# Second attention's scores: two heads at a time, the low key parts against the high query parts alone

## The chip, the cores and the metric

The kernel runs on one core of one Trainium2 chip. The metric is the device time of one execution in microseconds (us), as the median of several runs. The core has a matrix engine (PE, with its weight loads listed apart as PEld), a vector engine (DVE), a scalar engine (ACT), a pool engine (POOL) and a DMA queue issued by SP. Every engine takes its own instructions in program order; semaphores order them against each other.

## The reference

One layer on x of 16 sequences x 512 tokens x 256 channels, all in f32: `x = x + attention1(layernorm(x))`, then `x = x + block2(layernorm(x))`. Block 2 starts with the attention that the change touches:

```
q = (x @ Wq).reshape(b, t, H, D)                 # 16 heads of 64
q = concat(q_nope, rope(q_rope))                 # 32 + 32
k = concat(kv, rope(k_rope))                     # folded here: one key of 64, shared by all heads
att = softmax(causal(q . k / sqrt(64)))          # 512 x 512 scores for each head
y = (att @ v) @ Wo
x = x + y; then 8 experts (2 chosen) and one shared
```

## The kernel before

One pass of the loop handles one sequence (`sequence(b, last)` on each engine), 16 in all. The first attention, the projections, the second attention (`attend(b, 1, last)`) and the experts follow each other. The kernel is written engine by engine; the order on each engine is the order of the code, and `Signal` objects are semaphores with a count per sequence.

The second attention goes by units. A unit `u` is one group `g` of four heads and one tile `j` of 128 query tokens (`j` = 0, 1, 2, 3), so there are 4 x 4 = 16 units in a sequence. In turn PE makes the scores of unit u+1 (`score`), transposes the softmax numerators of unit u (`transpose_prob`, L670, 128x128 f32) and weighs the values of unit u-1 (`weigh_values`, L681, whose four heads stand in four 32-column tiles of the array). The scores of head `q` go to PSUM bank `q`. DVE takes the row maximum of each head (L1192), ACT the exponentials (L953), and PE's next scores into bank `q` wait for that head's exponentials (`prob_ready`).

Precision is kept by splitting. A query of 64 numbers is split in a high part (ACT, the copy into `stq` that signals `qh_ready`) and the low rest (DVE, L1324), stacked as 128 rows (high, low) by a transpose into `qt`. The high key part stands twice in `khh` (rows 0 to 63 and 64 to 127), the low key part twice in `kll`. `score` with `a == 1` issues three matmuls for a head: `qt` x `khh` (L657), `qt` x `kll` (L658), both with all 128 rows and m columns of keys, m = max(128(j+1), 256), and then the causal mask as a bf16 matmul of 128 columns (`ident16` x `mask16`, L659), whose end raises `s_psum`. Every matmul of the program has a weight load of its own.

Of the kernel before, what the change touches and what calls it, by code (L numbers as in the profile page):

```python
# [23 lines left out]
F32 = mybir.dt.float32  # L24
F32R = mybir.dt.float32r
BF16 = mybir.dt.bfloat16
ALU = mybir.AluOpType
# [3 lines left out]
P = 128  # L31
NB, L, C = 16, 512, 256
NT = L // P
KC = C // P
H = 16
D = C // H
HP = 32
G = 4
NG = H // G
M = 1  # L40
NM = G // M
# [4 lines left out]
DK = 2 * R  # L46
# [3 lines left out]
UNITS = NG * NT  # L50
# [23 lines left out]
def tile_of(u):  # L74
    return ORDER[u % NT]
# [24 lines left out]
def _build(nc, ctx, dram):  # L100
# [4 lines left out]
    def at(name, shape, dt, offset):  # L105
        return nc.alloc_sbuf_tensor_at(name, shape, dt, offset=offset)
# [23 lines left out]
    ident16 = new("ident16", [P, P], BF16)  # L130
    mask16 = new("mask16", [P, P], BF16)
# [53 lines left out]
    qkt = new("qkt", [SD, 2 * H, L], BF16)  # L185
    qt = at("qt", [P, H, L], F32R, region_q)
# [15 lines left out]
    qf = at("qf", [P, 2, 8, DK], F32, o + 8192)  # L202
    ta = at("ta", [P, 2, 8, R], F32, o + 12288)
    tb = at("tb", [P, 2, 8, R], F32, o + 14336)
    stq = at("stq", [P, 2, 8, 2, DK], F32R, o + 16384)

    va = new("va", [P, NT, H, HP], F32)
    xn0 = at("xn0", [P, NT, C], F32, place[0])
    sg = at("sg", [P, 2, L], F32, place[0])
    khh = new("khh", [P, L], F32R)  # L210
    kll = new("kll", [P, L], F32R)
# [27 lines left out]
    bank = [scores[:, i] for i in range(4)]  # L239
# [57 lines left out]
    qh_ready = Signal(sem("qh_ready"), 2 * NT)  # L297
    ql_ready = Signal(sem("ql_ready"), 2 * NT)
# [4 lines left out]
    s_psum = Signal(sem("s_psum"), 2 * NM * UNITS)  # L303
    negmax_ready = Signal(sem("negmax_ready"), 2 * NM * UNITS)
    prob_ready = Signal(sem("prob_ready"), 2 * G * UNITS)
# [255 lines left out]
    def _(pe):  # L561
        mm = nc.tensor.matmul
# [67 lines left out]
        def transpose_quad(b, n):  # L630
# [11 lines left out]
                                          stk[:, t % 2, quad * 8 + i].rearrange("p s d -> p (s d)"), ident16[:, :])  # L642
            ins.then_inc(stackt_psum.sem, 1)

        def score(b, a, u, part):
            g, j = u // NT, tile_of(u)
            n = (j + 1) * P
            for q in range(M * part, M * part + M):
                h = g * G + q
                if u > 0:  # L650
                    pe.wait_ge(prob_ready.sem, prob_ready.at(b, (a * UNITS + u - 1) * G + q + 1))
                if a == 0:
                    mm(bank[q][:, 0:n], qkt[:, h, j * P:(j + 1) * P], qkt[:, H + h, 0:n], start=True, stop=False)  # L653
                else:
                    m = max(n, 2 * P)
                    tok = qt[:, h, j * P:(j + 1) * P]
                    mm(bank[q][:, 0:m], tok, khh[:, 0:m], start=True, stop=False)  # L657
                    mm(bank[q][:, 0:m], tok, kll[:, 0:m], start=False, stop=False)  # L658
                ins = mm(bank[q][:, n - P:n], ident16[:, :], mask16[:, :], start=False, stop=True)  # L659
            ins.then_inc(s_psum.sem, 1)  # L660

# [31 lines left out]
        def attend(b, a, last):  # L693
            if a == 0 and b == 0:
                for part in range(NM):
                    score(b, a, 0, part)
            for u in range(UNITS):
                if u + 1 < UNITS:
                    for part in range(NM):
                        score(b, a, u + 1, part)  # L700
                if u == 0:
                    if a == 0:
                        pe.wait_ge(down_added.sem, down_added.at(b, 0))
                        pe.wait_ge(stackt_act.sem, stackt_act.at(b, 4 * NT))
                    else:
                        pe.wait_ge(qt_act.sem, qt_act.at(b, 2 * NT))
                        pe.wait_ge(qt_dve.sem, qt_dve.at(b, 2 * NT))
                        pe.wait_ge(vb_ready.sem, vb_ready.at(b, 1))
                early = EARLY[tile_of(u)]
                transpose_prob(b, a, u, range(early))  # L710
                if u > 0:
                    weigh_values(b, a, u - 1)
                    if u % NT == 0:
                        transpose_sums(b, a, u // NT - 1)
                transpose_prob(b, a, u, range(early, tile_of(u) + 1))
            transpose_sums(b, a, NG - 1)
            weigh_values(b, a, UNITS - 1)

            project_out(b, a, range(NG - 2))
            if a == 1 and not last:  # L720
                transpose_first(b + 1)
            project_out(b, a, range(NG - 2, NG))
# [87 lines left out]
        def sequence(b, last):  # L810
            if b == 0:
                pe.wait_ge(stackt_act.sem, stackt_act.at(b, 4 * NT))
            attend(b, 0, last)

            keep_busy(8, 6)
            transpose_tokens(b, 1, (0, 1))
            keep_busy(2, 6)
            hi_split(b, 1, 1)
            for n in range(2 * NT):
                project_q(b, n)  # L820
                if n == 0:
                    transpose_tokens(b, 1, (2, 3))
                if n == KV_STEP:
                    project_kv(b)
                if n > 1:
                    transpose_q(b, n - 2)
                if n == KV_STEP + 3:
                    pe.wait_ge(kv_copied.sem, kv_copied.at(b, 1))
                    settle(pe, pe_passed)
                    for t in range(NT):  # L830
                        ins = nc.tensor.transpose(bank[6][:, t * R:(t + 1) * R], kf[0:R, t * P:(t + 1) * P], ident[0:R, 0:R])
                    ins.then_inc(vb_psum.sem, 1)
            pe.wait_ge(kll_ready.sem, kll_ready.at(b, 1))
            pe.wait_ge(nope_ready.sem, nope_ready.at(b, 2 * NT))
            pe.wait_ge(rot_ready.sem, rot_ready.at(b, 2 * NT))
            for part in range(NM):
                score(b, 1, 0, part)
            transpose_q(b, 2 * NT - 2)
            transpose_q(b, 2 * NT - 1)
            attend(b, 1, last)  # L840

            if not last:
                for t in range(2):
                    project_qk(b + 1, t)
                    project_v(b + 1, t)
            transpose_tokens(b, 2)
            hi_split(b, 2)

            for m, (x_, w_) in enumerate(TERMS):
                if m == 2:  # L850
                    lo_split(b, 2)
                for k in range(KC):
                    ins = mm(bank[3][0:E, :], wgate[:, w_, k], XT[x_][:, k], start=m == 0 and k == 0, stop=m == 2 and k == KC - 1)
            ins.then_inc(gatet_psum.sem, 1)
            gate_up(b, 0, (0,))
            pe.wait_ge(gatet_copied.sem, gatet_copied.at(b, 1))
            settle(pe, pe_passed)
            for t in range(NT):
                ins = nc.tensor.transpose(bank[2][:, t * E:(t + 1) * E], lgt[0:E, t * P:(t + 1) * P], ident[0:E, 0:E])
            ins.then_inc(gate_psum.sem, 1)  # L860
            gate_up(b, 0, (1,))
            for e in range(NE + 1):
                if not last:
                    if e in PROJECT_AT:
                        project_qk(b + 1, PROJECT_AT[e])
                        project_v(b + 1, PROJECT_AT[e])
                    for n in QUADS_AT.get(e, ()):
                        transpose_quad(b + 1, n)
                if 1 <= e < NE:
                    spread_comb(b, e)  # L870
                if e + 1 < NE:
                    gate_up(b, e + 1)
                if e == NE and not last:
                    pe.wait_ge(hid_ready.sem, hid_ready.at(b, NE))
                    for part in range(NM):
                        score(b + 1, 0, 0, part)
                if e == 0:
                    transpose_comb(b)
                else:
                    down(b, e - 1)  # L880
# [14 lines left out]
    def _(act):  # L895

        def copy(out, in_, **k):
            return nc.scalar.activation(out, in_, ACT.Copy, **k)  # L898
# [95 lines left out]
        def sequence(b, last):  # L994
# [3 lines left out]
            for n in range(2 * NT + 3):  # L998
# [11 lines left out]
                if 1 <= n <= 2 * NT:  # L1010
                    act.wait_ge(rope_ready.sem, rope_ready.at(b, n))
                    act.wait_ge(nope_ready.sem, nope_ready.at(b, n))
                    if n >= 3:
                        act.wait_ge(qt_psum.sem, qt_psum.at(b, 2 * (n - 2)))
                    copy(stq[:, (n - 1) % 2, :, 0], qf[:, (n - 1) % 2]).then_inc(qh_ready.sem, 1)
                if n == 2 * NT:
                    for part in range(NM):
                        exps(b, 1, 0, part)
# [70 lines left out]
    def _(dve):  # L1089
# [194 lines left out]
        def sequence(b, last):  # L1284
# [24 lines left out]
            for n in range(2 * NT + 3):  # L1309
# [11 lines left out]
                if 1 <= n <= 2 * NT:  # L1321
                    dve.wait_ge(qh_ready.sem, qh_ready.at(b, n))
                    s = (n - 1) % 2
                    tt(stq[:, s, :, 1], qf[:, s], stq[:, s, :, 0].bitcast(F32), ALU.subtract).then_inc(ql_ready.sem, 1)  # L1324
                if 3 <= n < 3 + NT and not last:
                    ins = first_stats(b + 1, n - 3)
                if n == 3 + NT and not last:
# [148 lines left out]
```

## Time and profile before

| | |
|---|---|
| median of 3 runs | 3697.05 us (3696.23 to 3699.96) |
| the profiled execution's own time | 3699.16 us |
| its span, from first to last instruction | 3697.5 us |
| PE busy (matmul) | 3354.6 us, 91% of the span |
| PEld busy (weight load) | 2632.8 us, 71% |
| DVE, ACT, POOL busy | 75%, 65%, 29% |
| mean granted TensorE clock | 0.993 |
| matmuls L657, L658, and masks L659 (of both attentions) | 1024, 1024, 2048 |

A matmul's busy time includes the time until its result has left the array, and matmuls overlap. So what a matmul costs the stream is not its duration, but the distance from its start to that of the next one, called its turn below. Weight loads run beside the matmul ahead of them where they can.

### The profile page before, as it was taken

How to read it: one execution, taken by the hardware profiler on the slowest of the kernel's cores; microseconds unless marked ns; L12 is line 12 of the kernel's file. 1: busy time of each engine (PE TensorE's matmuls, PEld its weight loads, DVE VectorE, ACT ScalarE, POOL GpSimd, SP SyncE). 2: the span in 40 equal slices, each digit the busy share in tenths (PEclk: the TensorE clock that was granted, in tenths of full speed). 3: DMA queues.
4: the chain of work that ended last, by engine and by line, in shares of the span. 5: the costliest groups of instructions: out<-in, count | busy, mean ns of one | idle time of the engine just before them, and what ended most of it. 6: DMA issues, size and time to landing. Idle time of an engine off the chain costs nothing.

```text
span 3697.5 us, 82731 instructions
## 1 busy us (share of the span) xinstructions
PE 3354.6 (91%) x31744; PEld 2632.8 (71%) x31744; DVE 2763.8 (75%) x5950; ACT 2406.8 (65%) x6426; POOL 1085.9 (29%) x778
## 2 busy tenths in 40 slices
PE   2599999999999999999999999999999999999998
PEld 2477677776767777677776767777677776767776
DVE  3676877878777776877778777777877778777775
ACT  1666667666676766667666676766667666676764
POOL 0424222242412424222242412424222242412420
PEclk9799999999999999999999999999999999999999
DMA  3000000000000000000000000000000000000000
GB/s 80 1 7 1 13 2 7 7 7 7 1 13 2 7 7 1 13 1 7 7 7 7 1 13 2 7 7 1 13 2 7 7 7 7 2 13 2 7 2 7
DMA packets 33766, 28.95 MB, mean 8 GB/s; under 512 B 8864, under 2 KB 33312, under 8 KB 33376
## 3 DMA queue, kind: packets, MB, share of 16 engines
q1 hardware_dynamic: 33376, 23.68, 2.2%
q8 instruction: 253, 4.15, 0.5%
q14 instruction: 137, 1.12, 0.1%
HBM read 15.28 MB, written 8.39 MB: 6 GB/s over the span
## 4 chain that ended last, share of the span: by engine, by line
PE 71%; ACT 14%; DVE 10%; issue 3%; POOL 1%; SPq 1%; DMA 0%; ACTq 0%; POOLq 0%; DVEq 0%
PE bank L670 14%; PE scores L782 11%; PE bank L681 8%; ACT prob L953 6%; PE scores L657 5%; PE bank L806 5%; PE scores L733 4%; PE scores L658 4%; PE scores L756 3%; PE bank L617 3%; PE bank L641 3%; PE scores L659 3%; DVE negmax L1192 2%; ACT qkt L898 2%; PE scores L653 1%
## 5 line engine op out<-in xcount | busy, mean ns | idle before, releaser
L953 ACT ACTIVATE prob<-scores,negmax 128x128 f32<-128x128 f32 (+3 forms) x2048 | 1057.8, 535 | 186.3 <-DVE negmax L1192 180.6
L1192 DVE TENSOR_REDUCE negmax<-scores 128x1 f32<-128x128 f32 (+3 forms) x2048 | 872.6, 481 | 56.9 <-PE scores L659 42.4
L670 PE MATMUL bank<-ident,prob 128*128 128x128 f32 x5120 | 725.6, 279 | 50.6 <-DVE probt L1200 43.6
L1200 DVE COPY probt<-bank 128x512 f32<-128x512 f32 x896 | 596.1, 683 | 171.0 <-PE bank L670 165.3
L670 PEld LDWEIGHTS bank<-ident,prob 128*128 128x128 f32 x5120 | 544.1, 141 | 163.6 <-issue 66.6
L659 PE MATMUL scores<-mask,ident 128*128 128x128 bf16 x2048 | 438.1, 225 | 0.0
L953 ACT ACTIVATION_READ_ACCUMULATOR prob<-scores,negmax 128x1 f32 x2048 | 436.1, 213 | 0.0
L657 PE MATMUL scores<-khh,qt 128*128 128x256 f32 (+2 forms) x1024 | 416.3, 407 | 13.3 <-POOL kll L545 13.3
L486 POOL TENSOR_TENSOR otl<-onm,oth 128x512 fp32r<-128x512 f32 x96 | 122.6, 1277 | 888.8 <-ACT oth L898 888.8
L497 POOL TENSOR_TENSOR rq<-ssq,expo 128x32 f32<-128x32 f32 x64 | 359.9, 5632 | 39.6 <-DVE ssq L1163 39.6
L481 POOL COPY rexp<-rsum 128x512 f32<-128x512 f32 x128 | 78.0, 610 | 981.8 <-DVE rsum L1204 981.8
L898 ACT ACTIVATE probt<-bank 128x512 f32<-128x512 f32 x384 | 232.8, 606 | 198.8 <-PE bank L670 198.8
L782 PE MATMUL scores<-xth,wgu 128*128 128x512 f32 x1152 | 335.9, 413 | 0.0
L658 PE MATMUL scores<-kll,qt 128*128 128x256 f32 (+2 forms) x1024 | 331.4, 324 | 0.0
L659 PEld LDWEIGHTS scores<-mask,ident 128*128 128x128 bf16 x2048 | 199.5, 97 | 135.8 <-issue 110.5
L653 PE MATMUL scores<-qkt 96*128 96x128 bf16 (+3 forms) x1024 | 261.1, 304 | 29.3 <-ACT prob L953 6.6
L898 ACT ACTIVATE qkt<-bank 96x1024 bf16<-96x1024 bf16 x256 | 243.7, 1015 | 66.5 <-PE bank L641 66.5
L782 PEld LDWEIGHTS scores<-xth,wgu 128*128 128x128 f32 x1152 | 215.6, 189 | 41.8 <-issue 0.3
L641 PE MATMUL bank<-ident,stk 128*128 128x128 bf16 x2048 | 146.8, 224 | 87.1 <-ACT qkt L898 59.2
L657 PEld LDWEIGHTS scores<-khh,qt 128*128 128x128 f32 x1024 | 203.1, 198 | 18.8 <-POOL kll L545 17.1
L806 PE MATMUL bank<-wd,hidh 128*128 128x256 f32 x1152 | 211.5, 283 | 1.8 <-DVE hidl L1378 1.8
L1373 DVE TENSOR_TENSOR sg<-scores,sg 128x512 f32<-128x512 f32 x144 | 99.1, 688 | 134.0 <-ACT sg L1049 134.0
(187 smaller groups left out, 6654.6 us busy)
## 6 DMA issues: line engine op xcount, KB each, us to landing
x_in<-in_x_rows SPq DMA_DIRECT2D x16, 512.0 KB, 3.8
out_rows<-x SPq DMA_DIRECT2D x16, 512.0 KB, 2.9
r_gu<-in_wg SPq DMA_DIRECT2D x2, 512.0 KB, 5.0
r_gu<-in_wu SPq DMA_DIRECT2D x2, 512.0 KB, 5.7
r_d<-in_wd SPq DMA_DIRECT2D x1, 1024.0 KB, 7.1
r_wqt<-in_wq_nope_t SPq DMA_DIRECT2D x1, 512.0 KB, 6.7
r_wqr<-in_wq SPq DMA_DIRECT2D x2, 256.0 KB, 8.3
r_wob<-in_wo SPq DMA_DIRECT2D x1, 512.0 KB, 5.3
```

What stands on the lines that cost most here:

```text
L497: nc.gpsimd.tensor_tensor(rq[:, s], ssq[:, s], expo[:, 0:1].to_broadcast([P, 2 * H]), ALU.pow).then_inc(rq_ready.sem, 1)
L653: mm(bank[q][:, 0:n], qkt[:, h, j * P:(j + 1) * P], qkt[:, H + h, 0:n], start=True, stop=False)
L657: mm(bank[q][:, 0:m], tok, khh[:, 0:m], start=True, stop=False)
L658: mm(bank[q][:, 0:m], tok, kll[:, 0:m], start=False, stop=False)
L659: ins = mm(bank[q][:, n - P:n], ident16[:, :], mask16[:, :], start=False, stop=True)
L670: ins = nc.tensor.transpose(bank[4 + n % 2][:, q * P:(q + 1) * P], prob[:, u % 2, q, i * P:(i + 1) * P], ident[:, :])
L782: ins = mm(bank[2 * s + w][:, :], wgu[:, w_, e, k, w * I:(w + 1) * I], XT[x_][:, k], start=m == 0 and k == 0, stop=m == 2 and k == KC - 1)
L806: ins = mm(bank[4 + t // 2][:, (t % 2) * C:(t % 2 + 1) * C], (hidh, hidl)[x_][:, s, t * P:(t + 1) * P], wd[:, w_, e], start=e == 0 and m = ...
L898: return nc.scalar.activation(out, in_, ACT.Copy, **k)
L953: nc.scalar.activation(prob[:, u % 2, q, 0:n], bank[q][:, 0:n], ACT.Exp, bias=negmax[:, a, u, q:q + 1], accum_out=sums[:, a, u, q:q + 1]). ...
L1192: nc.vector.tensor_reduce(negmax[:, a, u, M * part:M * part + M], scores[:, M * part:M * part + M, 0:n], axis=AX.X, op=ALU.max, negate=Tru ...
L1200: nc.vector.tensor_copy(probt[:, u % 2, i], bank[4 + n % 2][:, :]).then_inc(probt_dve.sem, 1)
```

## The change

Three things change for the second attention. (1) In `stq`, odd heads are stacked (low, high) instead of (high, low): `high_low(s)` gives the views, and the ACT copy and the DVE subtraction write through them. (2) `score_pair` handles two heads: both products with `khh`, then both with `kll`, then both masks. (3) The product with `kll` takes only the 64 rows that hold the high query part: rows 0 to 63 for an even head and 64 to 127 for an odd one. The term low x low is left out of the scores. The first attention is as before.

```diff
+    def high_low(s):
+        v = stq[:, s].rearrange("p (i e) s d -> p i (e s) d", e=2)
+        return v[:, :, 0:4:3], v[:, :, 1:3]
+    def by_pairs(s):
+        return qf[:, s].rearrange("p (i e) d -> p i e d", e=2)
...
+        def score_unit(b, a, u):
+            if a == 0:
+                for part in range(NM):
+                    score(b, a, u, part)
+            else:
+                for pair in range(G // 2):
+                    score_pair(b, u, (2 * pair, 2 * pair + 1))
+        def score_pair(b, u, pair):
+            g, j = u // NT, tile_of(u)
+            n = (j + 1) * P
+            m = max(n, 2 * P)
+            for q in pair:
+                if u > 0:
+                    pe.wait_ge(prob_ready.sem, prob_ready.at(b, (UNITS + u - 1) * G + q + 1))
+                mm(bank[q][:, 0:m], qt[:, g * G + q, j * P:(j + 1) * P], khh[:, 0:m], start=True, stop=False)
+            for q in pair:
+                high = slice(q % 2 * DK, q % 2 * DK + DK)
+                mm(bank[q][:, 0:m], qt[high, g * G + q, j * P:(j + 1) * P], kll[high, 0:m], start=False, stop=False)
+            for q in pair:
+                mm(bank[q][:, n - P:n], ident16[:, :], mask16[:, :], start=False, stop=True).then_inc(s_psum.sem, 1)
...
-                    m = max(n, 2 * P)
-                    tok = qt[:, h, j * P:(j + 1) * P]
-                    mm(bank[q][:, 0:m], tok, khh[:, 0:m], start=True, stop=False)
-                    mm(bank[q][:, 0:m], tok, kll[:, 0:m], start=False, stop=False)
...
-                    copy(stq[:, (n - 1) % 2, :, 0], qf[:, (n - 1) % 2]).then_inc(qh_ready.sem, 1)
+                    copy(high_low((n - 1) % 2)[0], by_pairs((n - 1) % 2)).then_inc(qh_ready.sem, 1)
...
-                    tt(stq[:, s, :, 1], qf[:, s], stq[:, s, :, 0].bitcast(F32), ALU.subtract).then_inc(ql_ready.sem, 1)
+                    high, low = high_low(s)
+                    tt(low, by_pairs(s), high.bitcast(F32), ALU.subtract).then_inc(ql_ready.sem, 1)
```

On PE, in the second attention of the first sequence, the scores of a unit with m = 256 stood like this before, with the wait for the exponentials of the bank's last scores:

```order
L657 MATMUL scores<-khh,qt 128x256 [waits prob_ready]
L658 MATMUL scores<-kll,qt 128x256
L659 MATMUL scores<-mask_59,ident_58 128x128
L657 MATMUL scores<-khh,qt 128x256 [waits prob_ready]
L658 MATMUL scores<-kll,qt 128x256
L659 MATMUL scores<-mask_59,ident_58 128x128
L657 MATMUL scores<-khh,qt 128x256 [waits prob_ready]
L658 MATMUL scores<-kll,qt 128x256
L659 MATMUL scores<-mask_59,ident_58 128x128
```

At the same place now (x2 is two in a row; the shape shows what is written, so the 64 rows of the kll products don't appear in it):

```order
L668 MATMUL scores<-khh,qt 128x256 [waits prob_ready] x2
L671 MATMUL scores<-kll,qt 128x256 x2
L673 MATMUL scores<-mask_59,ident_58 128x128 x2
L668 MATMUL scores<-khh,qt 128x256 [waits prob_ready] x2
L671 MATMUL scores<-kll,qt 128x256 x2
L673 MATMUL scores<-mask_59,ident_58 128x128 x2
L694 MATMUL bank<-ident,prob 128x128 [waits probt_act,prob_ready]
```

The number of matmuls is the same. The products with khh moved together, the products with kll moved together behind them, and a pair's first mask moved behind its second head's products.

On ACT, the copies that split the query stood like this in the projection ahead of the second attention:

```order
L898 ACTIVATE qf<-scores 128x8x32
L898 ACTIVATE stq<-qf 128x8x64
L898 ACTIVATE qt<-bank 128x4x128
L898 ACTIVATE qf<-scores 128x8x32
L898 ACTIVATE stq<-qf 128x8x64
```

and now:

```order
L920 ACTIVATE qf<-scores 128x8x32
L920 ACTIVATE stq<-qf 128x4x2x64
L920 ACTIVATE qt<-bank 128x4x128
L920 ACTIVATE qf<-scores 128x8x32
L920 ACTIVATE stq<-qf 128x4x2x64
```

Nothing moved there; the copy writes as many numbers through a view with one more dimension.

## Rows read from the trace of the kernel before

**Rows 1.** The page: span.
```profile
span 3697.5 us, 82731 instructions
```
**Rows 2.** Stretch 915 to 931 us: PE, PEld, DVE, ACT, POOL busy, clock, DMA, GB/s.
```profile
915.00:931.00 16.00, 16.00 (x183) 12.46 (x180) 12.82 (x26) 11.85 (x40) 1.89 (x2) 1.00 0.01 2
```
**Rows 3.** PE's waits for other engines from 906 to 966 us.
```profile
PE bank L670 <- DVE probt L1200: 0.4, 1, 0.4
```
**Rows 4.** Timeline of PE, the transposes behind the scores of unit 0.
```profile
905.44 0.66 PE L769 MATMUL bank<-ident,stq 128*128 128x128 f32 x4 [1.55 <-ACT qt L898]
```
**Rows 5.** Timeline of PE, scores with 256 columns, then transposes and values (start, us).
```profile
920.22 0.23 PE L659 MATMUL scores<-mask,ident 128*128 128x128 bf16 x1
...
920.46 0.28 PE L658 MATMUL scores<-kll,qt 128*128 128x256 f32 x1
920.58 0.23 PE L659 MATMUL scores<-mask,ident 128*128 128x128 bf16 x1
...
921.01 0.60 PE L670 MATMUL bank<-ident,prob 128*128 128x128 f32 x4
921.55 1.08 PE L681 MATMUL bank<-probt,vb 128*32 128x128 f32 x32
```
**Rows 6.** Timeline of PE, scores with 384 columns.
```profile
924.36 0.23 PE L659 MATMUL scores<-mask,ident 128*128 128x128 bf16 x1
...
924.66 0.34 PE L658 MATMUL scores<-kll,qt 128*128 128x384 f32 x1
924.84 0.23 PE L659 MATMUL scores<-mask,ident 128*128 128x128 bf16 x1
```
**Rows 7.** Timeline of PE, scores with 512 columns.
```profile
926.76 0.23 PE L659 MATMUL scores<-mask,ident 128*128 128x128 bf16 x1
...
927.11 0.40 PE L658 MATMUL scores<-kll,qt 128*128 128x512 f32 x1
927.35 0.23 PE L659 MATMUL scores<-mask,ident 128*128 128x128 bf16 x1
```
**Rows 8.** Groups by shape (count, busy us, mean ns of one, idle before).
```profile
L681 PE MATMUL bank<-probt,vb 128*32 128x128 f32 x5120 | 192.9, 277 | 0.0
L681 PEld LDWEIGHTS bank<-probt,vb 128*32 128x32 f32 x5120 | 124.1, 109 | 36.4 <-issue 32.1
L756 PE MATMUL scores<-wq,xtl 128*128 128x512 f32 x256 | 80.4, 395 | 0.0
```
**Rows 9.** Timeline of PE around the only matmuls with 32 rows in the loop.
```profile
888.22 1.06 PE L769 MATMUL bank<-ident,stq 128*128 128x128 f32 x8
889.21 0.43 PE L831 MATMUL bank<-ident,kf 32*128 32x32 f32 x4
889.57 1.20 PE L756 MATMUL scores<-wq,xth 128*128 128x512 f32 x4
```
**Rows 10.** Timeline of PEld, loads in the stretch of rows 5.
```profile
921.54 0.81 PEld L681 LDWEIGHTS bank<-probt,vb 128*32 128x32 f32 x32 [0.17 <-issue]
922.56 0.42 PEld L690 LDWEIGHTS bank<-ident,rexp 128*128 128x128 f32 x4 [0.20 <-issue]
```
**Rows 11.** Timeline of PEld around the 32-row matmuls.
```profile
889.21 0.32 PEld L831 LDWEIGHTS bank<-ident,kf 32*128 32x128 f32 x4 [0.17 <-issue]
889.57 0.76 PEld L756 LDWEIGHTS scores<-wq,xth 128*128 128x128 f32 x4
```
**Rows 12.** Timeline of PEld, eight value loads behind the mask at 924.84.
```profile
925.00 0.16 PEld L681 LDWEIGHTS bank<-probt,vb 128*32 128x32 f32 x8
```
**Rows 13.** The writers of stq: duration min/median/max in ns.
```profile
L898 ACT ACTIVATE stq<-qf x128: 622/632/635, 217.5 to 3569.2; 128x512 fp32r<-128x512 f32 x128
L1324 DVE TENSOR_TENSOR stq<-qf,stq x128: 678/804/1231, 218.1 to 3569.8; 128x512 fp32r<-128x512 f32 x128
```
**Rows 14.** Timeline of ACT, end of the exponentials of a 512-column unit.
```profile
930.38 0.24 ACT L953 ACTIVATION_READ_ACCUMULATOR prob<-scores,negmax 128x1 f32 x1
```
**Rows 15.** Timeline of PE, the first scores of the unit after it.
```profile
930.57 0.36 PE L657 MATMUL scores<-khh,qt 128*128 128x256 f32 x1
```

More of the change, by code:

```diff
@@ L651, in score @@
                     pe.wait_ge(prob_ready.sem, prob_ready.at(b, (a * UNITS + u - 1) * G + q + 1))
-                if a == 0:
-                    mm(bank[q][:, 0:n], qkt[:, h, j * P:(j + 1) * P], qkt[:, H + h, 0:n], start=True, stop=False)
-                else:
-                    m = max(n, 2 * P)
-                    tok = qt[:, h, j * P:(j + 1) * P]
-                    mm(bank[q][:, 0:m], tok, khh[:, 0:m], start=True, stop=False)
-                    mm(bank[q][:, 0:m], tok, kll[:, 0:m], start=False, stop=False)
+                mm(bank[q][:, 0:n], qkt[:, h, j * P:(j + 1) * P], qkt[:, H + h, 0:n], start=True, stop=False)
                 ins = mm(bank[q][:, n - P:n], ident16[:, :], mask16[:, :], start=False, stop=True)
@@ L698, in attend @@
                 if u + 1 < UNITS:
-                    for part in range(NM):
-                        score(b, a, u + 1, part)
+                    score_unit(b, a, u + 1)
                 if u == 0:
@@ L835, in sequence @@
             pe.wait_ge(rot_ready.sem, rot_ready.at(b, 2 * NT))
-            for part in range(NM):
-                score(b, 1, 0, part)
+            score_unit(b, 1, 0)
             transpose_q(b, 2 * NT - 2)
```

## The prediction

> **What bounds the kernel now.** I read the page first: a span of 3697.5 us [rows 1], with PE the busiest engine by far. Then the busy time by engine inside one second attention: in 16 us PE is busy for all 16, DVE for 12.8, ACT for 11.9, and the granted clock is 1.00 [rows 2]. Then the waits of PE from 906 to 966 us, nearly all of that attention: one, of 0.4 us [rows 3]. So PE's stream sets the time here, and what a pair of heads costs more or less on PE goes into the total nearly whole. The exception is unit 0 of each sequence: behind its scores PE waits 1.55 us for ACT's copies [rows 4], and a few tenths more vanish in that. That leaves 15 units a sequence.
>
> The rest is read from starts on PE's timeline, for there a matmul costs its turn and not its duration. With m = 256 it takes 0.36 us from mask to mask, that is a head: 0.24 from the mask to the kll product and 0.12 from there to the next mask [rows 5]. With 384 columns it is 0.48 = 0.30 + 0.18 [rows 6], with 512 it is 0.59 = 0.35 + 0.24 [rows 7]. The khh product would need only the second figure, like the kll product of the same size; the 0.11 to 0.12 that the first figure has more are the mask's turn of some 0.05 and the rest of an f32 weight load that a mask is too short to cover.
>
> **What a change of the array's shape costs.** This is the term on which the forecast rests, because the new order changes from 128 rows to 64 and back in each pair. The program has such changes already. Four transposes start at 921.01 and last 0.60 together; one of this size lasts 0.277 [rows 8], so the last starts at 921.33. A transpose's turn is 0.11 (eight in 1.06, less 0.277, over seven [rows 9]), so it has streamed by 921.44 [rows 5]. The first load for 32-column tiles starts at 921.54 [rows 10]: 0.10 of nothing. Back again: 32 value matmuls from 921.55 for 1.08, the last starts at 922.35 and has streamed by 922.46; the next load starts at 922.56: 0.10 again [rows 5, 10]. In rows rather than columns there is one case: eight transposes from 888.22 for 1.06, the last through by 889.11, and the first load of 32 rows at 889.21: 0.10 [rows 9, 11]. Behind a change the first weight load is bare too: of four matmuls with 512 columns from 889.57, lasting 1.20 in all with 0.395 for one [rows 8], the fourth starts at 890.38; three turns of 0.23 back the first really starts at 889.68, 0.10 after its load [rows 9, 11].
>
> The Trainium skill (TensorEngine Tiling (Array Packing), Key Properties) says that a change of tiling mode, not of the tile alone, drains the engine. It speaks against this change; the waits above agree with it, and it gives no figure.
>
> **What the two halves gain.** Tiles side by side do run together: eight value loads on four column tiles take 0.16, and one of them lasts 0.109 [rows 8], so they start 0.007 apart [rows 12], and 32 value matmuls fit into 1.08, 0.026 each, where a lone one has a turn of 0.11 [rows 5]. No row shows two row tiles at once. I take the same for them: the second kll product starts 0.007, rounded to 0.01, behind the first. The other bound is that nothing overlaps: it starts a full turn later.
>
> **The sum for a pair**, from mask to mask. I take 0.01 off the turn ahead of a mask, since the mask's own load is in it: 0.11, 0.17 and 0.23.
> - to the start of the second khh product: 0.24, 0.30, 0.35 (it stands where the kll product stood)
> - its turn: 0.11, 0.17, 0.23
> - drain 0.10, bare load 0.10
> - both kll products: 0.12, 0.18, 0.24
> - drain 0.10, then the first mask's load and turn 0.06; the second mask closes the pair.
>
> That is 0.83, 1.01 and 1.18, against 0.72 (twice 0.36), 0.96 and 1.18 before: 0.11, 0.05 and 0.00 more. Of the 30 pairs that count in a sequence 14 have 256 columns, 8 have 384 and 8 have 512 (j = 0 and 1 are both padded to 256): 14 x 0.11 + 8 x 0.05 = 1.94 us, times 16 sequences 31 us. The sum is made against the profiled execution, whose own time of 3699 lies 2 us over its span and over the median; I put it on the median: 3697 + 31 = 3728.
>
> **What I cost at nothing.** The writers of `stq` take 632 ns on ACT and 804 on DVE [rows 13] for the same 512 numbers, in runs of 64 as before. Not less than nothing, and if the extra dimension cost a tenth, 8 ACT copies a sequence x 0.06 x 16 = 8 us, were they on the path. The masks behind both heads raise the first head's `s_psum` some 0.5 us later with 512 columns (its mask comes after 1.12 instead of 0.59). Queued behind it: the maxima, the exponentials, and PE's next scores into the same bank, which wait for them. The last exponentials end at 930.62 [rows 14]; the next unit's fourth khh product starts at 930.57 [rows 15] + 3 x 0.36 = 931.65. So 1.0 us is to spare, and half of it stays.
>
> **The rivals.**
> - The halves don't overlap, or only their loads come one after the other. For it: no row shows row tiles together, and full-array loads keep 0.11 apart. Loads in line: 480 pairs x 0.09 = 43 us more, 3771. No overlap at all: (14 x 0.10 + 8 x 0.16 + 8 x 0.22) x 16 = 71 more, 3799. Against it: the column tiles [rows 5, 12]. 17 in 100.
> - Faster, because a half needs no drain. The one case in rows [rows 11] has 32 rows, not 64. Then the drains and the bare load go (0.30 x 480 = 144 less): 3584. If only the way back to the mask is free, 48 less: 3680. The switch decides it: below 0.07 us a change of shape, instead of 0.10, the sum is negative. 7 in 100 for the whole, 12 for one way or a cheaper load.
> - The late first head stops PE. It needs the 1.0 us above to be gone; at 0.5 us in each of 15 units it would be 120 us, 3848. 4 in 100.
> - The dearer `stq` copies show: 3736, 5 in 100, inside the likeliest range.
>
> The Trainium skill's table for row tiling (the same page, Theoretical Speedup) promises up to 2x for 64 rows or fewer, which is the second rival with no price on it. No run here shows that.
>
> **How the numbers follow.** My forecast, with all terms within 0.03 us a pair, has 55 in 100 and 3715 to 3745 of its own. From 3680 to 3790 the range takes in loads in line and one free switch, and leaves out no overlap at all, no drain, and the stopped PE. A measurement here tells 0.2%, 7.4 us. Faster by more: the second rival's 19 and 6 from the forecast's tail, 25. Within: 10. Slower: 65.
>
> **What would show it.** Right: on PEld a wait for nothing of some 0.2 us ahead of the first kll load and the first mask load of each pair; the two kll loads and starts 0.01 apart; mask to mask over a pair 0.83, 1.01, 1.18; PE still without waits. Wrong: kll loads that start while the second khh product streams (no drain), or a second kll product that starts 0.1 us or a turn after the first, or PE waiting for ACT's `prob` in front of the khh products.

## The result, and the profile after

The changed kernel takes 3770.56 us (median of 4 runs, 3763.74 to 3774.29) against 3697.97 us for the kernel before beside it: a ratio of 1.0194, 95% interval 1.0176 to 1.0212. That is 73 us more. The forecast was slower by 31 us, with a range up to 3790.

First the page of the changed kernel, as [rows 1] for the kernel before:

```profile
span 3768.2 us, 82731 instructions
PE 3407.6 (90%) x31744; PEld 2596.7 (69%) x31744; DVE 2766.3 (73%) x5950; ACT 2418.4 (64%) x6426; POOL 1085.2 (29%) x778
```

DVE and ACT did what they did before, in a longer span. The writers of `stq` didn't change either (duration min/median/max in ns, as [rows 13]):

```profile
L920 ACT ACTIVATE stq<-qf x128: 620/632/637, 218.1 to 3634.1; 128x512 fp32r<-128x512 f32 x128
L1347 DVE TENSOR_TENSOR stq<-qf,stq x128: 678/800/1237, 218.7 to 3634.7; 128x512 fp32r<-128x512 f32 x128
```

Next the timeline of PE for a unit with 256 columns, as [rows 5] (start and duration in us; two in a row stand in one line):

```profile
933.97 0.48 PE L668 MATMUL scores<-khh,qt 128*128 128x256 f32 x2
934.39 0.39 PE L671 MATMUL scores<-kll,qt 64*128 64x256 f32 x2
934.70 0.29 PE L673 MATMUL scores<-mask,ident 128*128 128x128 bf16 x2
934.80 0.48 PE L668 MATMUL scores<-khh,qt 128*128 128x256 f32 x2
935.21 0.38 PE L671 MATMUL scores<-kll,qt 64*128 64x256 f32 x2
935.53 0.28 PE L673 MATMUL scores<-mask,ident 128*128 128x128 bf16 x2
```

and the weight loads of the same stretch:

```profile
934.38 0.19 PEld L671 LDWEIGHTS scores<-kll,qt 64*128 64x128 f32 x2
934.70 0.11 PEld L673 LDWEIGHTS scores<-mask,ident 128*128 128x128 bf16 x2
934.77 0.30 PEld L668 LDWEIGHTS scores<-khh,qt 128*128 128x128 f32 x2
935.21 0.19 PEld L671 LDWEIGHTS scores<-kll,qt 64*128 64x128 f32 x2
```

From mask to mask a pair takes 0.83 us (934.70 to 935.53), as the sum had it. The two 64-row loads take 0.19 together, as long as one (0.184 in its group), so they start within a few nanoseconds; both kll products last 0.38 together, where one lasts 0.381 in its group. Taken singly in this trace, the second product of a pair starts 3 to 4 ns behind the first, and so does its load. The halves do run side by side. The Trainium skill (TensorE: Matmul & The Clock Gate, Part 3) draws tiles of 32 rows that start about 4 ns apart; these tiles of 64 rows agree with it. The second khh product really starts at 934.17 (0.20 after the first's record, as in the kernel before). It streams for 0.11, then nothing happens for 0.10, and at 934.38 the 64-row loads begin. From there to the mask it is 0.32: the bare load 0.10, the product 0.11, and 0.10 of nothing again, the drain.

With 512 columns, a pair and what follows it, as [rows 7] (PE; the bracket is the idle time ahead of it and who ended it):

```profile
942.14 0.28 PE L673 MATMUL scores<-mask,ident 128*128 128x128 bf16 x2
942.23 0.71 PE L668 MATMUL scores<-khh,qt 128*128 128x512 f32 x2
942.88 0.50 PE L671 MATMUL scores<-kll,qt 64*128 64x512 f32 x2
943.31 0.28 PE L673 MATMUL scores<-mask,ident 128*128 128x128 bf16 x2
943.43 0.61 PE L694 MATMUL bank<-ident,prob 128*128 128x128 f32 x4
943.97 0.64 PE L705 MATMUL bank<-probt,vb 128*32 128x128 f32 x16
944.54 0.66 PE L694 MATMUL bank<-ident,prob 128*128 128x128 f32 x4
945.54 0.66 PE L694 MATMUL bank<-ident,prob 128*128 128x128 f32 x4 [0.34 <-DVE probt L1222]
945.95 0.48 PE L668 MATMUL scores<-khh,qt 128*128 128x256 f32 x2
```

and DVE at that time:

```profile
942.41 2.48 DVE L1214 TENSOR_REDUCE negmax<-scores 128x1 f32<-128x512 f32 x4 [0.80 <-PE scores L673]
944.81 1.27 DVE L1222 COPY probt<-bank 128x512 f32<-128x512 f32 x2
```

The pair takes 1.17 us (942.14 to 943.31), as worked out. But four transposes start at 944.54 and the next four only at 945.54: 1.00, where four turns are 0.44. Eight in a row stood there before. The late four need bank 5, which DVE empties (`probt<-bank`) behind the four maxima, and the maxima start at 942.41, 0.96 before the last mask (943.37, 0.06 behind the first of its pair). In the kernel before they started 1.51 before it (927.02 and 928.53). DVE and PE stood there like this:

```profile
927.02 2.48 DVE L1192 TENSOR_REDUCE negmax<-scores 128x1 f32<-128x512 f32 x4 [0.28 <-PE scores L659]
929.42 0.68 DVE L1200 COPY probt<-bank 128x512 f32<-128x512 f32 x1
```

```profile
929.72 1.10 PE L670 MATMUL bank<-ident,prob 128*128 128x128 f32 x8
```

There the copy ended at 930.10. Of the eight transposes the fifth is the first that needs the copied bank; taken singly in the trace, it started at 930.21, some 0.1 later. Of that 0.05 is the way from a copy's end to the transpose it releases (in the changed kernel the first copy ends at 945.49 and the transposes start at 945.54). So the spare time was some 0.05 us, against maxima that start 0.55 later. From last mask to next khh product it was 2.04 (928.53 to 930.57), and is 2.58 now (943.37 to 945.95): some 0.55 in each of 64 units, 35 us. That is a little more than 0.55 less the spare time, because the first transpose behind a wait has a turn of 0.16 and not 0.11.

### The profile page after: what moved, and what is told of

The parts are those of the page before. It is cut to its first block, busy times and chain, and to the rows that moved or that the text cites. A ratio compares the mean times of both kernels' runs of the same rounds, so it can differ in the third digit from the quotient of the medians.

```text
span 3768.2 us, 82731 instructions
## 1 busy us (share of the span) xinstructions
PE 3407.6 (90%) x31744; PEld 2596.7 (69%) x31744; DVE 2766.3 (73%) x5950; ACT 2418.4 (64%) x6426; POOL 1085.2 (29%) x778
## 4 chain that ended last, share of the span: by engine, by line
PE 66%; ACT 14%; DVE 14%; issue 4%; POOL 1%; SPq 1%; DMA 0%; ACTq 0%; POOLq 0%; DVEq 0%
PE bank L694 13%; PE scores L805 11%; PE bank L705 7%; ACT prob L975 6%; DVE negmax L1214 5%; PE bank L829 5%; PE scores L756 4%; PE scores L668 4%; PE scores L671 4%; PE scores L779 3%; PE bank L625 3%; PE bank L649 2%; PE scores L673 2%; ACT qkt L920 2%; DVE probt L1222 2%
## 5 line engine op out<-in xcount | busy, mean ns | idle before, releaser
L694 PE MATMUL bank<-ident,prob 128*128 128x128 f32 x5120 | 744.8, 280 | 66.8 <-DVE probt L1222 58.7
L975 ACT ACTIVATION_READ_ACCUMULATOR prob<-scores,negmax 128x1 f32 x2048 | 427.8, 209 | 0.0
L668 PE MATMUL scores<-khh,qt 128*128 128x256 f32 (+2 forms) x1024 | 303.1, 374 | 13.4 <-POOL kll L553 13.2
L671 PE MATMUL scores<-kll,qt 64*128 64x256 f32 (+2 forms) x1024 | 219.2, 425 | 0.0
L683 PE MATMUL scores<-mask,ident 128*128 128x128 bf16 x1024 | 202.4, 221 | 0.0
L829 PEld LDWEIGHTS bank<-wd,hidh 128*128 128x128 f32 x1152 | 185.2, 189 | 12.0 <-ACT hidh L920 2.1
L705 PE MATMUL bank<-probt,va 128*32 128x128 f32 x5120 | 193.1, 278 | 0.0
```

The source lines that it names most:

```text
L668: mm(bank[q][:, 0:m], qt[:, g * G + q, j * P:(j + 1) * P], khh[:, 0:m], start=True, stop=False)
L671: mm(bank[q][:, 0:m], qt[high, g * G + q, j * P:(j + 1) * P], kll[high, 0:m], start=False, stop=False)
L694: ins = nc.tensor.transpose(bank[4 + n % 2][:, q * P:(q + 1) * P], prob[:, u % 2, q, i * P:(i + 1) * P], ident[:, :])
L705: ins = mm(bank[6][q * HP:(q + 1) * HP, j * P:(j + 1) * P], val, probt[:, u % 2, i, q * P:(q + 1) * P], start=i == 0, stop=i == j)
L829: ins = mm(bank[4 + t // 2][:, (t % 2) * C:(t % 2 + 1) * C], (hidh, hidl)[x_][:, s, t * P:(t + 1) * P], wd[:, w_, e], start=e == 0 and m = ...
L975: nc.scalar.activation(prob[:, u % 2, q, 0:n], bank[q][:, 0:n], ACT.Exp, bias=negmax[:, a, u, q:q + 1], accum_out=sums[:, a, u, q:q + 1]). ...
```

## The experiments

Theory A, after the two traces: the 73 us have two causes. The pairs with their changes of shape are one, near the forecast; the copy of a transposed block that queues behind later maxima is the other. Theory B: all of it comes from the array, and the wait for DVE is only where it shows.

**Pairs with 128 rows.** No change of shape is left:

```diff
-                high = slice(q % 2 * DK, q % 2 * DK + DK)
-                mm(bank[q][:, 0:m], qt[high, g * G + q, j * P:(j + 1) * P], kll[high, 0:m], start=False, stop=False)
+                mm(bank[q][:, 0:m], qt[:, g * G + q, j * P:(j + 1) * P], kll[:, 0:m], start=False, stop=False)
```

> The changed kernel's order by pairs, but the kll products take all 128 rows, so the array never changes its shape. Theory A (two causes: the changes of shape inside a pair, some 33 us, and some 35 us of PE waiting in front of the last transposes behind the 512-column scores, because the pair's first mask comes 0.5 us later and DVE's copy of a transposed block is queued behind the maxima): the pairs get shorter than before, 0.66, 0.90 and 1.13 us against 0.73, 0.96 and 1.18, but the wait stays with some 0.5 us in each of 64 units; 3704 us. Theory B (all of the 73 us comes from the changes of shape, and the wait for DVE is only where they show): no wait, about 3667 us.

Measured: 3722.59 us, ratio 1.0062 (1.0047 to 1.0077). B falls: with no change of shape left in the scores, the kernel is still slower than before. Its timeline on PE from a 384-column unit on:

```profile
929.03 0.59 PE L668 MATMUL scores<-khh,qt 128*128 128x384 f32 x2
...
929.91 0.85 PE L668 MATMUL scores<-khh,qt 128*128 128x384 f32 x2
...
933.39 0.28 PE L673 MATMUL scores<-mask,ident 128*128 128x128 bf16 x2
...
934.50 0.28 PE L673 MATMUL scores<-mask,ident 128*128 128x128 bf16 x2
...
935.73 0.66 PE L694 MATMUL bank<-ident,prob 128*128 128x128 f32 x4
936.79 0.44 PE L694 MATMUL bank<-ident,prob 128*128 128x128 f32 x2 [0.40 <-DVE probt L1222]
```

The 512-column pair takes 1.11 instead of 1.18, and the wait for DVE is there (1.06 between the two sets of transposes). But A's 3704 was 19 us too low. The first two lines say why: two khh products of the same size take 0.59 in the first pair and 0.85 in the second. The second one of the later pair waits 0.26. The changed kernel has it too, smaller, 0.14 (PE):

```profile
937.61 0.59 PE L668 MATMUL scores<-khh,qt 128*128 128x384 f32 x2
...
938.60 0.73 PE L668 MATMUL scores<-khh,qt 128*128 128x384 f32 x2
```

Its timeline of ACT shows what that product, the fourth head's, waits for:

```profile
936.25 0.20 ACT L975 ACTIVATION_READ_ACCUMULATOR prob<-scores,negmax 128x1 f32 x1
937.33 0.60 ACT L920 ACTIVATE osb<-bank 128x512 f32<-128x512 f32 x1 [0.88 <-PE bank L705]
...
938.63 0.21 ACT L975 ACTIVATION_READ_ACCUMULATOR prob<-scores,negmax 128x1 f32 x1
```

The exponentials of the third and fourth head stand behind the copy `osb` of the weighed values, for which ACT waits 0.88 us. The fourth head's end at 938.84, and in the order by pairs the fourth khh product comes earlier than it did, right behind the third.

**A third bank.** The sixth transposed block of a group goes to bank 7, idle at that time:

```diff
+                if third_bank(a, n):          # a == 1 and n % 10 == 5
+                    pe.wait_ge(onm_ready.sem, onm_ready.at(b, a * NG + n // 10))
-                if n >= 2:
+                elif n >= 2:
                     pe.wait_ge(*block_copied(b, a, n - 2))
```

On the changed kernel:

> The changed kernel, and in the second attention the sixth transposed block of each group (the last one of the 384-column unit) goes to PSUM bank 7, so PE needs no wait for DVE's copy out of bank 5 there. Theory A: the wait of 0.55 us in 64 units goes, 35 us less, 3736 us, with the pairs unchanged at 0.82, 1.04 and 1.18 us. Theory B: no more than 7 us less than the changed kernel, 3763 to 3771.

Measured: 3743.09 us, ratio 1.0120 (1.0105 to 1.0135), 27 us under the changed kernel. The 512-column pairs keep their 1.17 (937.48 to 938.65) and eight transposes stand together again (PE):

```profile
937.48 0.29 PE L679 MATMUL scores<-mask,ident 128*128 128x128 bf16 x2
...
938.65 0.28 PE L679 MATMUL scores<-mask,ident 128*128 128x128 bf16 x2
...
939.88 1.09 PE L702 MATMUL bank<-ident,prob 128*128 128x128 f32 x8
```

The copy behind the maxima was the wait. By the starts in the traces a sequence without a fall of the clock got 2.1 us shorter (226.4 to 224.3), 34 us in 16. The time shows 8 us less than the 35 expected, and the clock took that back (below). In the profiled run of this kernel the second attention of seven sequences took 1.1 or 2.5 us longer than in the others, 11 us in all, each with a fall of the granted clock in it; in that of the changed kernel three did, 3 us in all.

On the kernel before:

> The kernel before with the same third bank for the sixth block. Both theories: no change, 3690 to 3704 us, since PE doesn't wait there in the kernel before.

Measured: 3698.24 us, 0.9996 (0.9987 to 1.0005). No change: the bank was no limit before.

**The layout alone**, with order and rows as before:

> The new layout of stq alone (odd heads low, high) with the order and the 128-row products of the kernel before. Theory A and B: no change, 3690 to 3704 us. Rival: the writers of stq with one more dimension are slower and show, up to 3706 us.

Measured: 3697.71 us, 0.9997 (0.9987 to 1.0007). The writes through four dimensions cost nothing that shows.

**Both heads in one half** (`high = slice(0, DK)`, and `stq` written as before):

> The changed kernel, but both heads of a pair use rows 0 to 63 (stq laid out as before), so the two kll products can't run side by side. Theory A (side by side at full rate): the second one comes a turn later, 4.4 us a sequence more in the scores, less 0.2 us of waiting in each 512-column unit: about 3827 us. Rival (the halves share the array at half rate each, and side by side gains nothing): about 3770, as the changed kernel.

Measured: 3853.28 us, ratio 1.0417 (1.0383 to 1.0452). The two 512-column kll products last 0.73 together, against 0.50 in two halves:

```profile
968.37 0.28 PE L673 MATMUL scores<-mask,ident 128*128 128x128 bf16 x2
...
969.10 0.73 PE L671 MATMUL scores<-kll,qt 64*128 64x512 f32 x2
969.76 0.28 PE L673 MATMUL scores<-mask,ident 128*128 128x128 bf16 x2
```

A pair takes 1.39 us from mask to mask, against 1.17. So the halves side by side gain a full turn, each at full rate. Most of the rest over 3827 is the clock: in the profiled run (3876 us) five sequences took 237 us and one 234.6, the others 230.5, and the last one's second attention was 6.6 us longer too, 44 us in all. The fastest of the four runs, whose mean granted clock was 0.993 as in the kernel before, took 3835.57. The last 5 to 9 us over 3827 have no cause shown. One fall of the clock, with the stretch ahead and the one behind (PE, PEld, DVE, ACT, POOL busy, then the granted clock):

```profile
705.00:708.40 3.40, 2.27 (x15) 1.68 (x16) 1.68 (x4) 1.85 (x7) 0.00 (x0) 0.97 0.00 0
708.50:725.50 17.00, 17.00 (x79) 10.97 (x78) 8.05 (x14) 8.21 (x26) 0.00 (x0) 0.51 0.00 1
726.00:741.00 15.00, 15.00 (x160) 10.50 (x160) 10.87 (x24) 10.16 (x34) 1.89 (x2) 1.00 0.00 1
```

**Halves for each head** (`score_pair(b, u, (q,))` for each q):

> The order of the kernel before (khh, kll, mask for each head) with 64-row kll products in the new layout. A pair's switches are then paid by each head, with nothing side by side and without a late first mask. Theory A (a switch to 64 rows and back costs 0.10 + 0.10 + 0.10 us whatever stands around it): 0.29 us in each of 960 heads, 278 us more, 3976 us. Rival (the price belongs to pairs, or the drain back is the mask's own): 0.10 to 0.20 a head, 3793 to 3889.

Measured: 3973.61 us, ratio 1.0746 (1.0730 to 1.0763). By the ratio that is 276 us over the kernel before, in 960 heads 0.29 each. So a trip to 64 rows and back costs 0.3 us for a head alone as it does for a pair. With two heads for one trip, half of it is paid for each; side by side gives back 0.11 to 0.23 a pair.

**128 rows, third bank:**

> Order by pairs with 128-row kll products, and the third bank for the sixth transposed block. Theory A: the wait of 0.60 us behind the 512-column scores goes (39 us in 64 units), and the shorter pairs are left: 3684 us, 0.4% under the kernel before. If the wait only moves to the next bank or to the exponentials: 3715 to 3723.

Measured: 3693.71 us, ratio 0.9983 (0.9974 to 0.9992). 29 us less than without the third bank, not 39: the wait went, but its profiled run has seven falls of the clock in second attentions, some 1 us each, and that of the kernel without the third bank has none.

**Exponentials ahead of `osb`.** In `attend` of ACT, for the second attention:

```diff
-                if u % NT == 1 and u > NT:
+                if a == 0 and u % NT == 1 and u > NT:
                     copy_out(b, a, u // NT - 1)
...
+                if a == 1 and u % NT == 1 and u > NT:
+                    copy_out(b, a, u // NT - 1)
                 for i in mine:
```

On the changed kernel with the third bank:

> The changed kernel with the third bank, and ACT makes all four heads' exponentials of a group's 256-column unit before it copies the weighed values out (osb), not two before and two behind. Theory A, now with three parts (25 us for the pairs themselves, 35 us for the copy queued behind the maxima, 12 us for the second head of a 384-column unit that waits for those exponentials): the third part goes as well, 12 us less than with the third bank alone, 3731 us; some of it is the lower clock at the start of the attention, which stays. Rival (the wait in the 384-column unit is the array's, not ACT's): 3743, as with the third bank alone.

Measured: 3731.76 us, ratio 1.0093 (1.0079 to 1.0106). That is 11 us less than with the third bank alone and near the 12, but not all of one cause. By the starts in the two traces a 384-column unit of the second to fourth group got 0.13 us shorter, 6 us in 48 units; 4 us more come from fewer and shorter falls of the clock (six with 7 us, after seven with 11). In the first group, which has no `osb` ahead, the second head still waits 0.30 us; no run took that out.

On the kernel before:

> The kernel before with ACT's exponentials ahead of osb. No wait of PE for them is there to be taken out, so no change: 3690 to 3704 us. If osb then comes too late for PE's next values or DVE's product, slower.

Measured: 3698.06 us, 1.0002 (0.9993 to 1.0011). No change.

On 128 rows with the third bank:

> Order by pairs, 128-row kll products, third bank, exponentials ahead of osb. Theory A: the wait of 0.24 us in 64 units goes too, 15 us less than with the third bank alone (3694): 3679 us. Rival: the wait goes to the values or to the maxima, 3690 to 3697.

Measured: 3681.38 us, ratio 0.9958 (0.9945 to 0.9970). 12 us less where 15 were expected: 0.25 us in 48 units, not 64, for the same reason.

**A filler for the clock.** In the traces with falls inside the second attention they start 2 to 7 us after its first scores. In the kernels by pairs it is 5 to 7 us, just behind the place where PE has waited 1.55 us for ACT. Four matmuls of 512 columns go ahead of that wait; they write bank 6, which nobody reads then:

```diff
+                if m == 4 * NT - 1:
+                    pe.wait_ge(vb_ready.sem, vb_ready.at(b, 1))
+                    keep_busy(4, 6)
                 if m >= 3:
```

> The same, with four bf16 matmuls of 512 columns into bank 6 ahead of PE's wait for ACT at the start of the second attention, where the granted clock fell in some sequences 5 to 7 us after the first scores. If the falls come of the idle time there, they go, and with them about 1 us each in 7 sequences: 7 us less than without the filler, unless the filler delays the copies behind it (0.9 us at most, 14 us in all).

Measured: 3672.30 us, ratio 0.9933 (0.9919 to 0.9946), 9 us under the same kernel without it. The windows without the filler and then with it:

```profile
454.80:459.90 5.10, 3.37 (x29) 2.84 (x30) 3.60 (x13) 3.11 (x11) 1.94 (x2) 1.00 0.00 0
459.90:463.30 3.40, 3.40 (x19) 3.21 (x18) 2.23 (x6) 1.54 (x7) 0.00 (x0) 0.50 0.02 5
```

```profile
454.80:459.90 5.10, 4.23 (x34) 3.19 (x33) 3.40 (x14) 3.11 (x11) 1.65 (x2) 1.00 0.01 3
459.90:463.30 3.40, 3.38 (x25) 2.62 (x24) 2.98 (x7) 1.93 (x8) 0.00 (x0) 1.00 0.00 0
```

Same stretch, and the same work but for the filler; PE was busy 3.37 of 5.10 us ahead of it in the first and 4.23 in the second, and only in the first is the granted clock at 0.50, that is 1.2 GHz. With the filler no second attention of the profiled run has a fall. The mean granted clock of the five runs rose from 0.988 to 0.990 without it to 0.992 to 0.993 with it.

On the changed kernel with both waits out:

> The changed kernel with the third bank, the exponentials ahead of osb, and the filler at the start of the second attention. Theory A: the falls of the clock go (6 in the profiled run without the filler, 1.1 us each, 7 us), and what is left over the kernel before is the price of the pairs with their switches alone, 25 us: 3723 us. If the falls come of the 64-row products themselves, the filler changes nothing: 3731.

Measured: 3726.07 us, ratio 1.0073 (1.0056 to 1.0090). No second attention of the profiled run has a fall here either. This is the changed kernel with all that was found taken out but the pairs and the first group's wait: 26 us over the kernel before.

## Why the prediction was half right

**Right: the sign and the array.** PE sets the time, and a change of shape costs 0.10 us of drain each way and 0.10 of bare load; the 128-to-32-column and 128-to-32-row changes of the kernel before gave the price for 64 rows. The pairs came out at 0.82, 1.00 (where no head waits) and 1.17, as medians over the trace, against 0.83, 1.01 and 1.18 in the sum. The same medians of the kernel before are 0.73, 0.96 and 1.19, against 0.72, 0.96 and 1.18. So this term was 10 us too large: it is 31 us in the sum, while of the 26 left at the end some 5 are the wait of the first group and 21 the pairs. Hundredths of a microsecond, 480 times over, make that difference. That the halves run side by side, taken over from column tiles, was right too; the rivals of loads in line and of no overlap fall, though the time of the first, 3771, is the one that was measured. A time that fits is no evidence for the mechanism.

**Wrong: "What I cost at nothing", the masks behind both heads.** The prediction worked out that the first head's `s_psum` comes 0.5 us later, and named what is queued behind it: "the maxima, the exponentials, and PE's next scores". It followed that one way, found 1.0 us to spare, and gave the stopped PE 4 in 100. It left out what else stands behind the maxima on DVE: the copy of the transposed block, for which PE's next transposes into bank 5 wait. That way had some 0.05 us to spare, visible in the kernel before, and nearly all of the 0.55 went through: 35 us that the forecast put at nothing.

**Missing: the wait of a pair's second head.** In the order by pairs the fourth head's khh product stands right behind the third's, with 384 columns at 1.00 + 0.18 us instead of 3 x 0.48, some 0.25 earlier, while the exponentials that it waits for stayed where they were. The prediction checked that way only for the scores behind a 512-column unit. In three 384-column units of a sequence that waits 0.13 us, 6 us in all, and in the first 0.30, the 5 us above.

**Missing: the clock.** The granted clock was said to be 1.00 in the attention [rows 2], and there it is; but the start, where unit 0's extra cost was to "vanish" in PE's wait for ACT, became a place where it falls in some sequences. The filler is worth 6 us on the changed kernel with the waits out.

Taken out one after another, the third bank gave 27, the exponentials 11 and the filler 6, and 26 were left: 71 of the 73 us. The remaining 2 lie in the kernel before, which took 3697.97 beside the first of these runs and 3699.90 beside the last. Without the clock, by the starts in the traces: 34 for the copy behind the maxima, 7 for the exponentials, 26 left, and 3 for the falls of the changed kernel's own profiled run.

The order by pairs without the halves, with the two waits and the falls taken out, gives 3672.3 us, 25 under the kernel before. Its pairs take 0.66, 0.88 and 1.11 us, against 0.73, 0.96 and 1.19. That fits one reason, which no run tested by itself: the load that a mask is too short to cover is paid once for two heads instead of twice.

## What to carry to other kernels

Half the array for half the work pays only if it saves more than the trip there and back, here 0.3 us. Two products side by side save one turn, 0.11 to 0.23 us, so by these figures one trip must carry at least two such couples of 512 columns or three of 256 (an estimate; no run tried it). When an order makes a signal later, follow every instruction behind the one that waits, on its own engine, to whoever waits for those; the smallest spare time on any of these ways counts, and here the short way (a copy, a bank) had 0.05 us and the long one 1.0. Take a suspected wait out of the kernel before as well: both fixes here are worth nothing there, and 27 and 11 us in the changed kernel.

## What the hardware showed that I had not expected

The granted clock falls to its lower level a few us after the first scores of the second attention, in some sequences and not in others with the same work. Mostly it stays there for 3.4 us, which costs some 1 us. In the changed kernel with the third bank it did so twice for 6.8, which costs 2.5, and in `one_half` mostly for 17, which costs 6.6. It did so in kernels in which the unit's scores are longer as well as shorter than before. The profiled run of the kernel before has no such fall. That of the pairs with 128 rows has none either, but seven with the third bank, though the first scores are the same. Four matmuls of filler in the 1.55 us wait left none in the profiled runs of both kernels in which it was tried. Why the clock falls in some sequences and not in others, and why a fall lasts 3.4 us in one kernel and 17 in another, stays open.
